# Two-layer decoder with a routed mixture: who normalises the experts' rows, double-buffered split weights, biases loaded earlier, routing steps at other places in the order

## The reference

```python
gates = softmax(tokens @ wg); expert_idx = argmax(gates)      # 2048 tokens, 8 experts
# the first 320 tokens of each expert are kept, in their order
h   = relu(dispatched @ w1[e] + b1[e])                        # 320 x 256 -> 320 x 1024
out = (h @ w2[e] + b2[e]) * gate                              # 320 x 1024 -> 320 x 256
x   = layernorm(x + scattered(out))
```

## Time and profile before

| | us |
|---|---|
| median of 3 runs | 1764.5 (1758.85 to 1768.97) |
| the profiled execution's own time | 1766.83 |
| its span | 1765.0 |
| attention part, from the start to the first instruction of the second part | 1557.0 |
| routed mixture, from there to the end | 208.0 |
| TensorE busy over the span | 1547.5 (88%) |
| VectorE, ScalarE, GpSimd busy | 930.1, 849.5, 428.5 |

### The profile page before, as it was taken

One profiled execution on the slowest core, in us unless ns is written; L12 is line 12 of the kernel. 1 busy time (PEld: TensorE's weight loads), 2 busy tenths in 40 slices (PEclk: granted clock), 3 DMA queues, 4 the chain that ended last, 5 costly groups with the idle time before them and its releaser, 6 DMA issues. The chain is left out here.

```text
span 1765.0 us, 30531 instructions
## 1 busy us (share of the span) xinstructions
PE 1547.5 (88%) x12064; PEld 1169.3 (66%) x12064; DVE 930.1 (53%) x1915; ACT 849.5 (48%) x1419; POOL 428.5 (24%) x586
## 2 busy tenths in 40 slices
PE   2799999988899999999999999879999999657776
PEld 2577766655567887888888778556555554356766
DVE  4456667655544334152343443666677877455454
ACT  0154556655445554544545546345444344255454
POOL 0002455512110011020220220322212323414444
PEclk9699999999889999999999999989999999879988
DMA  4656776634231202112022022226735430043321
GB/s 91 92 86 123 149 133 131 116 76 66 38 53 28 38 8 42 25 19 37 2 37 37 2 43 37 37 56 119 166 68 105 102 62 26 23 171 109 121 94 42
DMA packets 98893, 123.99 MB, mean 70 GB/s; under 512 B 8284, under 2 KB 88899, under 8 KB 96192
## 3 DMA queue, kind: packets, MB, share of 16 engines
q1 hardware_dynamic: 96240, 117.44, 33.8%
q0 software_dynamic: 1792, 3.94, 0.7%
q10 hardware_dynamic: 720, 0.66, 0.1%
HBM read 48.86 MB, written 9.51 MB: 33 GB/s over the span
## 5 line engine op out<-in xcount | busy, mean ns | idle before, releaser
L999 DVE TENSOR_REDUCE mx<-mslot 128x4 f32<-128x1024 f32 x192 | 234.5, 1222 | 219.3 <-PE mslot L557 218.3
L825 ACT ACTIVATE probs<-eslot 128x1024 f32<-128x1024 f32 x192 | 196.8, 1025 | 169.5 <-PE eslot L582 141.8
L997 DVE TENSOR_REDUCE mx<-mslot 128x2 f32<-128x256 f32 (+1 forms) x256 | 130.5, 552 | 224.7 <-PE mslot L557 223.6
L1203 POOL TENSOR_SCALAR ave<-amv 128x2 f32<-128x2 f32 x64 | 16.8, 262 | 930.9 <-DVE amv L922 574.7
L582 PE MATMUL eslot<-stack 50*128 50x256 f32 (+2 forms) x1280 | 158.2, 326 | 9.1 <-ACT probs L825 8.3
L582 PEld LDWEIGHTS eslot<-stack 50*128 50x128 f32 (+1 forms) x1280 | 98.7, 191 | 98.0 <-issue 67.6
L557 PE MATMUL mslot<-stack 48*128 48x256 f32 (+2 forms) x1280 | 142.4, 302 | 10.8 <-DMA stack<-split 9.7
L823 ACT ACTIVATE probs<-eslot 128x512 f32<-128x512 f32 (+1 forms) x256 | 111.6, 488 | 73.9 <-PE eslot L582 72.8
L597 PE MATMUL bank<-probs,v 128*32 128x256 f32 (+1 forms) x2048 | 131.2, 369 | 0.0
L645 PE MATMUL bank<-hidden,l 128*128 128x256 f32 x512 | 114.0, 381 | 0.0
L557 PEld LDWEIGHTS mslot<-stack 48*128 48x128 f32 (+1 forms) x1280 | 102.3, 196 | 15.0 <-issue 10.8
(11 more groups left out here) (212 smaller groups left out, 3229.2 us busy)
## 6 DMA issues: line engine op xcount, KB each, us to landing
stack<-split SPq DMA_DIRECT2D x240, 256.0 KB
w<-in_w SPq DMA_DIRECT2D x16, 1024.0 KB, 5.0
slot_rows<-hTf SPq DMA_DIRECT2D x4, 650.0 KB, 8.7
slot_rows_sb<-slot_rows SPq DMA_DIRECT2D x4, 650.0 KB, 8.4
expert_rows<-slot_rows SPq DMA_DIRECT2D x8, 260.0 KB, 2.7
xb<-in_x SPq DMA_DIRECT2D x8, 256.0 KB, 8.9
l<-in_l SPq DMA_DIRECT2D x2, 1024.0 KB, 10.2
qk<-in_ctx SPq DMA_DIRECT2D x8, 256.0 KB, 5.9
```

The lines of the kernel that those rows point to most:

```text
L825: e = act.activation(PR[:, k, :, :, :].rearrange("p a k q -> p (a k q)"), ps[:, :, :, :].rearrange("p a k q -> p (a k q)"), ACT.Exp, scale ...
L997: a = dve.tensor_reduce(MX[:, qt, :, p], ps[:, :, qt, 0:(qt + 1) * P], AX.X, ALU.max)
L999: a = dve.tensor_reduce(MX[:, :, :, p].rearrange("p q a -> p a q"), ps[:, :, :, :], AX.X, ALU.max)
```

## The change

Four things. VectorE normalises the experts' rows with one instruction per row group (mean and inverse root as scalars), GpSimd no longer computes a shift, and ScalarE's `even` is gone. The split weights have two buffers each, so their high part waits for expert e - 2; the second pair of `hid` buffers lies in the memory of the turned slot rows. The biases are loaded in layer 4 beside the first expert's weights, into memory of the small mixture; at the end of the attention part SP waits for the last scatter and the last "out". The routing steps have other numbers, and in the experts' loop the order on ScalarE, VectorE and GpSimd differs.

```diff
-    ROUTE = {30: ["even"], 31: ["even rows", "xT"], 32: ["out", "logits"], 33: ["chances", "rank"], 34: ["scatter"]}
+    ROUTE = {30: ["even", "xT"], 31: ["even rows"], 32: ["logits"], 33: ["chances"], 34: ["rank"], 38: ["scatter", "out"]}
...
+                for dst, name in ((b1, "b1"), (b2, "b2")):
+                    sp.dma_start(dst, t[name]).then_inc(*shared["biases_in"](name))
...
+        sp.wait_ge(*base_out.at(UNITS - 1))
+        sp.wait_ge(*scattered.at(B * TT - 1))
...
-    w1_high = sb("w1_high", [P, CC, DFF], F32R)
+    w1_high = [sb(f"w1_high{k}", [P, CC, DFF], F32R) for k in range(2)]
...
+    retired = rows[:, :, :].rearrange("p n c -> p (n c)").bitcast(F32R)
+    hid_low, hid_high = [[sb(name, [P, FC, CAP], F32R), retired[:, k * FC * CAP:(k + 1) * FC * CAP]
+                          .rearrange("p (f s) -> p f s", f=FC)] for k, name in enumerate(("hid_low", "hid_high"))]
...
-        for dst, name in ((b1, "b1"), (b2, "b2")):
-            sp.dma_start(dst.ap(), t[name]).then_inc(*const_in(name))
...
-            if e >= 1:
-                act.wait_ge(*(pe_up.at(e - 1, FC - 1) if name == "w1" else pe_down.at(e - 1, 2)))
+            if e >= 2:
+                act.wait_ge(*(pe_up.at(e - 2, FC - 1) if name == "w1" else pe_down.at(e - 2, 2)))
+                act.wait_ge(*dve_low.at(name, e - 2))
...
             for f in range(FC):
                 up(e, f)
-                if e >= 1 and f == 1:
-                    even(e - 1, 2)
-                if e + 1 < E1 and f == 5:
-                    gated_bias(e + 1)
             if e + 1 < E1:
                 weights_high("w1", e + 1)
-            even(e, 0)
-            if e + 1 < E1:
                 weights_high("w2", e + 1)
-            even(e, 1)
-        even(E1 - 1, 2)
+                gated_bias(e + 1)
...
+        def even(e, j):
+
+            m, k = CH[j][1], e % 2
+            dve.wait_ge(*pool_root.at(e, j))
+            dve.tensor_scalar(eo[k][0:m, j, :], eo[k][0:m, j, :], mv[0:m, k, j, 0:1], rstd[0:m, k, j:j + 1],
+                              ALU.subtract, ALU.mult).then_inc(*dve_even(e, j))
...
             if e + 1 < E1:
                 weights_low("w1", e + 1)
-            for j in range(3):
-                combine(e, j)
+            combine(e, 0)
             if e + 1 < E1:
                 weights_low("w2", e + 1)
+            combine(e, 1)
+            even(e, 0)
+            combine(e, 2)
+            even(e, 1)
+            even(e, 2)
...
         for e in range(E1):
-            if e + 1 < E1:
-                add_bias(e + 1)
             inverse_root(e, 0)
             inverse_root(e, 1)
             put_rows(e, 0)
             inverse_root(e, 2)
             put_rows(e, 1)
+            if e + 1 < E1:
+                add_bias(e + 1)
             put_rows(e, 2)
```

More of the change, by code:

```diff
@@ L78, in at, with bias_tiles @@
         return self.sem, self.known.get(key, self.step)
+def bias_tiles(spare):
+    return (spare[:, E1 * C:E1 * C + E1 * DFF // P].rearrange("p (e f) -> p e f", e=E1),
+            spare[:, 0:E1 * C].rearrange("p (e c) -> p e c", e=E1))
 def build(nc, t, known):
@@ L88, in build @@
         sb = lambda name, shape: outer.enter_context(nc.sbuf_tensor(name, shape, F32))
-        shared = {"ident": sb("ident", [P, P]), "w1": sb("w1", [P, CC, DFF]), "w2": sb("w2", [P, DFF // P, C])}
-        for name in ("w1_in", "w2_in", "scattered", "base_out"):
+        shared = {"ident": sb("ident", [P, P]), "w1": sb("w1", [P, CC, DFF]), "w2": sb("w2", [P, DFF // P, C]),
+                  "spare": sb("spare", [P, 16 * KEEP])}
+        for name in ("w1_in", "w2_in", "biases_in", "scattered", "base_out"):
             shared[name] = Signal(name, outer.enter_context(nc.semaphore(name)), known, 16)
@@ L225, in attention_layers @@
     down3 = sb("down3", [P, 2, C])
-    downs = sb("downs", [P, 4, 4, KEEP])
+    downs = shared["spare"][:, :].rearrange("p (e k c) -> p e k c", e=4, k=4)
+    b1, b2 = bias_tiles(shared["spare"])
     XR = [sb(f"xb{b}", [P, TT, WIDE]) for b in range(B)]
@@ L1441, in routed_mixture @@
     half = sb("neg_half2", [P, 3])
-    b1 = sb("b1", [P, E1, FC])
-    b2 = sb("b2", [P, E1, C])
-    w1_high = sb("w1_high", [P, CC, DFF], F32R)
-    w1_low = sb("w1_low", [P, CC, DFF], F32R)
-    w2_high = sb("w2_high", [P, FC, C], F32R)
-    w2_low = sb("w2_low", [P, FC, C], F32R)
+    b1, b2 = bias_tiles(shared["spare"])
+    biases_in = shared["biases_in"]
+    w1_high = [sb(f"w1_high{k}", [P, CC, DFF], F32R) for k in range(2)]
+    w1_low = [sb(f"w1_low{k}", [P, CC, DFF], F32R) for k in range(2)]
+    w2_high = [sb(f"w2_high{k}", [P, FC, C], F32R) for k in range(2)]
+    w2_low = [sb(f"w2_low{k}", [P, FC, C], F32R) for k in range(2)]
     rows = sb("slot_rows_sb", [P, ST, WIDE])
@@ L1451, in routed_mixture @@
     hid = sb("hid", [P, 3, CAP])
-    hid_low = [sb(f"hid_low{k}", [P, FC, CAP], F32R) for k in range(2)]
-    hid_high = [sb(f"hid_high{k}", [P, FC, CAP], F32R) for k in range(2)]
+    retired = rows[:, :, :].rearrange("p n c -> p (n c)").bitcast(F32R)
+    hid_low, hid_high = [[sb(name, [P, FC, CAP], F32R), retired[:, k * FC * CAP:(k + 1) * FC * CAP]
+                          .rearrange("p (f s) -> p f s", f=FC)] for k, name in enumerate(("hid_low", "hid_high"))]
     xe = [sb(f"expert_rows{k}", [P, 3, WIDE]) for k in range(2)]
@@ L1479, in routed_mixture @@
     dve_stat = signal("dve_stat")
+    dve_even = signal("dve_even")
     dve_chain = signal("dve_chain2")
     pool_bias = signal("pool_bias")
-    pool_even = signal("pool_even")
+    pool_root = signal("pool_root")
     pool_chain = signal("pool_chain2")
@@ L1491, in _, with weights @@
     def _(sp):
-        for dst, name in ((b1, "b1"), (b2, "b2")):
-            sp.dma_start(dst.ap(), t[name]).then_inc(*const_in(name))
[L1495 to L1498, removed]
+        def weights(name, e):
+            sp.wait_ge(*dve_low.at(name, e - 1))
+            sp.dma_start({"w1": w1, "w2": w2}[name][:, :, :], t[name][e]).then_inc(*w_in[name](e))
         def slot_rows(e):
@@ L1517, in _ @@
             if e + 1 < E1:
-                weights(e + 1)
+                weights("w1", e + 1)
+                weights("w2", e + 1)
                 slot_rows(e + 1)
@@ L1551, in _ @@
                 for ci in range(CC):
-                    mm = products(UPS[ups % 3][:, 0:CAP], (w1_high[:, ci, fs], w1_low[:, ci, fs]),
+                    mm = products(UPS[ups % 3][:, 0:CAP], (w1_high[e % 2][:, ci, fs], w1_low[e % 2][:, ci, fs]),
                                   (xs_high[:, ci, at], xs_low[:, ci, at]), ci == 0, ci == CC - 1)
@@ L1572, in weights_high @@
         def weights_high(name, e):
-            high, full = {"w1": (w1_high, w1), "w2": (w2_high, w2)}[name]
+            high, full = {"w1": (w1_high[e % 2], w1), "w2": (w2_high[e % 2], w2)}[name]
             act.wait_ge(*w_in[name].at(e))
-            if e >= 1:
-                act.wait_ge(*(pe_up.at(e - 1, FC - 1) if name == "w1" else pe_down.at(e - 1, 2)))
+            if e >= 2:
+                act.wait_ge(*(pe_up.at(e - 2, FC - 1) if name == "w1" else pe_down.at(e - 2, 2)))
+                act.wait_ge(*dve_low.at(name, e - 2))
             act.activation(high[:, :, :], full[:, :, :], ACT.Copy).then_inc(*act_high(name, e))
@@ L1589, in up @@
             a.then_inc(*act_up(e, f))
[L1591 to L1596, removed]
         def gated_bias(e):
@@ L1612, in _ @@
                            TURN[n % 4][:, :].rearrange("p (a b) -> p a b", a=CC), ACT.Copy).then_inc(*act_rows(n))
-        act.wait_ge(*const_in.at("b2"))
+        act.wait_ge(*biases_in.at("b2"))
         gated_bias(0)
@@ L1636, in weights_low @@
         def weights_low(name, e):
-            low, high, full = {"w1": (w1_low, w1_high, w1), "w2": (w2_low, w2_high, w2)}[name]
+            low, high, full = {"w1": (w1_low[e % 2], w1_high[e % 2], w1), "w2": (w2_low[e % 2], w2_high[e % 2], w2)}[name]
             dve.wait_ge(*act_high.at(name, e))
@@ L1696, in inverse_root @@
             if e >= 2:
[L1697 to L1701, removed]
+                pool.wait_ge(*dve_even.at(e - 2, j))
+            then(pool.tensor_scalar(ve[0:m, k, j:j + 1], mv[0:m, k, j, 1:2], 1e-5, None, ALU.add))
+            pool.tensor_tensor(rstd[0:m, k, j:j + 1], ve[0:m, k, j:j + 1], half[0:m, 0:1], ALU.pow)\
+                .then_inc(*pool_root(e, j))
         def put_rows(e, j):
             m, k = CH[j][1], e % 2
-            pool.wait_ge(*act_even.at(e, j))
+            pool.wait_ge(*dve_even.at(e, j))
             pool.indirect_dma_start(t["out"], bass.IndirectOffsetOnAxis(ap=xe[k][0:m, j, TOKEN:TOKEN + 1].bitcast(U32), axis=0),
                                     eo[k][0:m, j, :], None, bounds_check=B * S - 1, oob_is_err=False).then_inc(*written[j](e))
-        pool.wait_ge(*const_in.at("b2"))
+        pool.wait_ge(*biases_in.at("b2"))
         pool.wait_ge(*base_out.at(UNITS - 1))
```

11 lines of the change are left out of this document (5 added, 6 removed).

## The result

The changed kernel takes 1694.64 us (median of 4 runs, 1684.3 to 1696.44) against 1766.74 before (4 runs): ratio 0.9592, 95% interval 0.9558 to 0.9626. Six further executions gave 0.9605 (0.9561 to 0.9649). The forecast was 1711, range 1695 to 1736: right in sign, kind and place, too small in size.

What follows compares the result with a forecast made beforehand. A put-landing-load round trip bound each expert at 25.06 us; first `hid_low` at 1567.4, expert 0 18.5, six periods of 18.0, last expert 19.3, less 2 in layer 4: span 1711.2, forecast 1711, range 1695 to 1736.

Steps and rivals of the forecast that it cites:

- I add 0.7 ... I take 18.0: Experts' loop: 0.7 us added to 17.3 for slower `hid_low` and TensorE's wait at chunk 6; period 18.0, from 17.0 to 20.0.
- I take -2: Middle of layer 4: earlier logits, freed GpSimd and SP, against extra biases; 2 us saved, bounds +4 and -6.
- The round trip: Experts' rows: put, landing, load; hidden by about 1 us. Rival that it binds: period 20 to 22, 1725 to 1737, chance 0.20.
- the loop ScalarE, VectorE, GpSimd: Experts' part after the change: chain from one first `hid_low` to the next sets the period, 17.3 us by rows.
- The extra 1 MB: Middle of layer 4: biases loaded early there, costing 0 to 3 us.
- The seam: Between attention and experts, units 38 and 39: earlier "xT" saves 2.8 us at unit 38 and 2.5 at unit 39.
- 1.5 us lost: End of attention: engines wait for the last scatter's landing, 4.8 us after its start against 3.3; bounds 0 and 3.
- From the slots' transfer to the first `hid_low`: Start of the experts' part: slots' transfer starts at 1553.2, VectorE's low parts end at 1559.7, first `hid_low` at 1567.4.
- The tail: Last expert: from its first `hid_low` through the last put to the kernel's end, 19.3 us.
- TensorE as the bound: Experts' loop rival: TensorE's 15.1 us of work binds; period 15.3 to 16.5, time about 1698; chance 0.12.
- The lower clock: Experts' products rival: TensorE's clock stays low after the chunk 6 wait; 28.1 us per expert, 1799; chance 0.04.
- the change doesn't free the loop: Experts' loop rival: some other wait holds the period at 25, only the seam's gain is left, 1755; chance 0.04.

Runs made afterwards that it cites:

- More work on TensorE: Changed kernel plus 8 products of 256 columns per expert into an unused bank, 0.9 us; period 16.93, whole time 1703.3 us (one run).
- the variants with 213.8: Six variants differing from the changed kernel only in the routed mixture; 213.8 us each from unit 31's residual to unit 38's.
- the order alone: Kernel before with only the routing steps at their new numbers; ratio 0.9941 (0.9908 to 0.9975).
- the second execution: Changed kernel run once more, unaltered, as base of other variants; 1696.15 us (median of 6), ratio 0.9605, period 16.93.
- the later evens: Changed kernel with evens of groups 1 and 2 behind the next expert's third `hid_low`, last put ahead of `add_bias`; 1690.5 us, ratio 0.9592, period 16.39.
- the root is moved: Changed kernel with GpSimd's root of group 2 ahead of the put of group 0; ratio 0.9656 (0.9604 to 0.9709), mean period 16.94.
- more work on VectorE: Changed kernel plus one 128x2048 memset per expert ahead of combine of group 0; period 20.0, whole time 1716.0 us (one run).
- one buffer: Changed kernel with one buffer per split weight, high parts waiting for expert e - 1; period 23.4, whole time 1744.5 us (one run).

## Why the forecast was right, and where it was wrong

The mechanism was right, sizes were wrong. The step that failed most is the last of the loop, "I add 0.7 ... I take 18.0": the period measured 16.94. Next come the price of the order in layer 4, "I take -2", which measured -6.8, and, outside the working, 4.4 us of spread between executions.

**What bounds, and what takes its place.** Right. The round trip left the loop; the loop ScalarE, VectorE, GpSimd took over, with the instructions in the order given. By rows I had 17.3; measured 16.94. Of the difference 0.26 lies at the put of group 0, which starts 0.19 behind the root of group 1, not 0.45. The root of group 0 came as forecast: its first instruction took 2.18 us beside w2's low part and the root was done before combine of group 1 ended. More work on TensorE left the period, more on VectorE moved it. Undone one by one were the second buffers and the evens' place; the moves of `gated_bias` and of `add_bias` were not tried by themselves.

```profile
1668.24 2.18 POOL L1707 TENSOR_SCALAR ve<-mv 128x1 f32<-128x1 f32 x1 [3.97 <-DVE mv L1653]
```

**"I add 0.7 ... I take 18.0".** Wrong, and the largest miss: 6 x 1.06 = 6.4 us, and 0.7 in the first period (17.84, not 18.5). Neither ground applied. `hid_low` does stretch beside `add_bias`, but ScalarE's chunks still come 0.82 apart, and VectorE then waits another 0.9 for ScalarE ahead of w1's low part; and TensorE waits 1.1, not 2, and keeps its clock at 1.00.

**"I take -2" in layer 4.** Wrong by 4.8: 6.8 us from 31 to 38 (6.2 in the variants with 213.8). The forecast gave each of units 32 to 37 half a microsecond, from no row. In the traces units 32 to 35 give 0.9 together, but units 36 and 37 give 2.6 each: it had no term for TensorE's waits for `hTf` there and for the products at the lower level behind them. The extra 1 MB, priced at 0 to 3, cost nothing that shows: 213.8 with the order alone, 213.2 to 213.8 with the biases as well.

**The seam.** Units 38 and 39: 5.3 forecast, 5.6 measured (3.0 and 2.6). "1.5 us lost" for the landing: 0. The 3.5 us in it came from a put beside a 1 MB load; the last scatter lands 2.4 us after its start, ahead of the meeting at 3.36. From the slots' transfer to the first `hid_low` 15.3, not 14.2: the last quarter of the slots lands 9.4 us after its issue and the rounds end with it, not with VectorE's low parts.

**The tail.** 19.3 forecast, 19.6 measured (1674.99 to 1694.6).

**What no step had.** Unit 31's residual is 4.4 us earlier in this execution than in the one of before, ahead of anything that acts by then. Over all traces it comes no earlier in the kernels with the biases loaded early than in the others (means 1295.2 and 1294.1): this part is luck of the two executions. With it the terms (unit 31, layer 4, seam, landing, slots to `hid_low`, first period, six periods, tail) make 4.4 + 4.8 + 0.3 + 1.4 - 1.1 + 0.7 + 6.4 - 0.3 = 16.6, which is what lies between the forecast's span, 1711.2, and the measured 1694.6. In the second execution this term is 0.6, the others as here.

**The rivals.** TensorE as the bound: not in the changed kernel, but 0.5 us below its period, as the later evens showed. The round trip: hidden in the changed kernel, but it binds in some experts once the root is moved. The lower clock: not at this wait; it came in the variants where TensorE waited up to 3.6 us in one go. That the change doesn't free the loop: no, 25.06 became 16.94; but with either part undone it is 23.3 to 23.4.

**The range.** Its lower end, 1695, stood for TensorE as the bound. The loop at its own rows (17.3, 4.9 us less over seven periods) and the lower bound in layer 4 (4 less) come to 1702, inside it. What went beyond is mainly the loop another 2.2 us below its rows, the landing that cost nothing, and the 4.4 us at unit 31; the spread of single executions, 16 us there, had no place in the range.

## What to carry to other kernels

Sum the loop from rows and leave it at that: an added allowance needs a row of its own, as a rounding up in a loop counts once per turn. A landing that was read beside a large load says little on one beside nothing. When a wait of TensorE goes, price the products behind it at full clock too. Where two waits of one loop are removed together, undoing either can give back most of it, here four fifths, so they are worth building and judging together.

## What the runs showed of the hardware

- TensorE waited 1.1 us per expert at a granted clock of 1.00. From 1600 to 1640 it was granted 0.96 with up to 3.6 us of wait per expert (more work on VectorE), and 0.83 with 3.6 and 1.5 us (one buffer). Behind a wait of 3.56 us two chunks came 1.60 us apart instead of 0.82.
- In layer 4, with three waits of 1.3 to 2.6 us in units 36 to 38, TensorE was granted 0.94 over these units, and 1.00 without them.
- An indirect put took 1.0 us alone, 2.4 beside three `hid_low` and 2.96 beside a low part of 2.29.
- The last scatter landed 2.4 us after its start, and waiting for it added nothing to a meeting of all engines 3.36 us behind that start.
- Up to unit 31, behind instructions that no variant changes, executions came up to 16 us apart, while the same layer 4 behind it took 213.2 to 213.8 us in eight executions.
